# Attention with seven instead of eight lead steps, and its shared units at other places

## The reference

```
x = x + tanh(g_xattn) * attention(layernorm(x), ctx)     # x: 8 x 512 x 256, ctx: 8 x 512 x 192
x = x + tanh(g_ffn)   * ffn(layernorm(x))
attention: q, k, v = projections; s = clip(q k^T / 4, -1e4, 1e4); softmax(s) v; @ Wo + bo
ffn: gates = logits * (logits >= kth); h = gelu(x w1 + b1); y = h w2 + b2; out = sum_e y_e gates_e
```

## Time and profile before

| | us |
|---|---|
| median of three runs | 1897.73 |
| lowest and highest | 1895.09, 1897.74 |
| profiled execution, its own time | 1896.23 |
| its span | 1894.4 |
| attention in it | 93.0 to 516.1 |
| TensorE, VectorE, ScalarE busy over the span | 1862.6, 1291.1, 1277.7 |

### The profile page before, as it was taken

One profiled execution on the slowest core, in us unless ns is written; L12 is line 12 of the kernel. 1 busy time (PEld: TensorE's weight loads), 2 busy tenths in 40 slices (PEclk: granted clock), 3 DMA queues, 4 the chain that ended last, 5 costly groups with the idle time before them and its releaser, 6 DMA issues.

```text
span 1894.4 us, 25738 instructions
## 1 busy us (share of the span) xinstructions
PE 1862.6 (98%) x8868; PEld 1349.0 (71%) x8868; DVE 1291.1 (68%) x2279; ACT 1277.7 (67%) x2145; POOL 146.9 (8%) x327
## 2 busy tenths in 40 slices
PE   7999999999999999999999999999999999999998
PEld 6844444444478777887888788788878888887886
DVE  6789999999666665656556666755665676556555
ACT  4447778777855556767666676766667676666665
POOL 6201101111135200000000000000000000000000
PEclk9969999999999999999999999999999999999999
DMA  8933333233113254333232333233233423222321
GB/s 284 374 81 84 87 91 88 79 88 110 38 50 129 107 210 151 119 117 110 90 111 89 133 138 124 95 112 112 89 112 129 151 93 117 111 90 89 121 101 58
DMA packets 97245, 220.84 MB, mean 117 GB/s; under 512 B 31314, under 2 KB 49492, under 8 KB 87892
## 3 DMA queue, kind: packets, MB, share of 16 engines
q1 hardware_dynamic: 97108, 219.12, 33.5%
HBM read 178.57 MB, written 40.24 MB: 116 GB/s over the span
## 4 chain that ended last, share of the span: by engine, by line
PE 89%; ACT 3%; DVE 2%; issue 1%; POOL 0%; ACTq 0%; DVEq 0%; POOLq 0%
PE ps_y L2169 32%; PE ps_h L2116 28%; PE ps_t L862 7%; PE ps_o L873 6%; PE ps_h L2089 5%; PE ps_y L2101 4%; PE ps_s L851 2%; PE ps_m L898 2%; PE ps_m L884 1%; ACT w_raw L1170 1%; DVE low L1007 1%; PE ps_m L890 0%; ACT gelu L2366 0%; PE ps_m L919 0%; PE ps_m L905 0%
## 5 line engine op out<-in xcount | busy, mean ns | idle before, releaser
L2469 DVE TENSOR_TENSOR h_lo<-gelu,h_hi 128x512 fp32r<-128x512 f32 x512 | 352.8, 693 | 437.0 <-ACT h_hi L2369 405.7
L2116 PE MATMUL ps_h<-x_hi,w_pair 128*128 128x512 f32 x1568 | 562.3, 392 | 1.8 <-ACT gelu L2366 0.8
L2366 ACT ACTIVATE gelu<-early,b 128x512 f32<-128x512 f32 x336 | 243.2, 724 | 229.5 <-DVE early L2618 220.7
L2116 PEld LDWEIGHTS ps_h<-x_hi,w_pair 128*128 128x128 f32 x1568 | 294.3, 188 | 78.3 <-issue 6.0
L1007 DVE TENSOR_REDUCE low<-ps_s 128x1 f32<-128x512 f32 x512 | 322.1, 681 | 26.1 <-PE ps_s L851 23.1
L2369 ACT ACTIVATE h_hi<-gelu 128x512 fp32r<-128x512 f32 x448 | 283.5, 633 | 41.9 <-ACT gelu L2366 1.1
L2116 PE MATMUL ps_h<-x_lo,w_pair 128*128 128x512 f32 x784 | 309.4, 395 | 0.0
L2618 DVE TENSOR_TENSOR early<-ps_h,copy 128x512 f32<-128x512 f32 x336 | 230.5, 686 | 49.4 <-PE ps_h L2116 49.4
L1170 ACT ACTIVATE probs_T<-ps_t 128x512 f32<-128x512 f32 x384 | 206.4, 594 | 45.5 <-PE ps_t L862 44.6
L851 PE MATMUL ps_s<-k_st,q_st 48*128 48x512 f32 x512 | 205.0, 481 | 3.2 <-SPq L755 2.0
L2169 PE MATMUL ps_y<-h_hi,w_lo 128*128 128x512 f32 x512 | 202.7, 396 | 0.0
(11 more groups left out here) (263 smaller groups left out, 2536.4 us busy)
## 6 DMA issues: line engine op xcount, KB each, us to landing
x_hi<-blocks_scratch SPq DMA_DIRECT2D x28, 1024.0 KB, 5.2
x_lo<-blocks_scratch SPq DMA_DIRECT2D x28, 1024.0 KB, 8.8
x_hi<-blocks_scratch SPq DMA_DIRECT2D x28, 768.0 KB, 6.7
x_lo<-blocks_scratch SPq DMA_DIRECT2D x28, 768.0 KB, 10.2
gate<-gates_scratch SPq DMA_DIRECT2D x64, 256.0 KB, 3.2
q_st<-q_scratch SPq DMA_DIRECT2D x192, 64.0 KB, 2.3
k_st<-k_scratch SPq DMA_DIRECT2D x192, 64.0 KB, 2.3
k_scratch<-k_hl SPq DMA_DIRECT2D x8, 1024.0 KB, 5.6
```

Source lines behind the costliest of these rows:

```text
L2116: mm = pe.matmul(bank, w[wp], x[xp], start=start and n == 0, stop=n == 2, skip_group_check=not start)
L2366: act.activation(gelu[:, c % GELUS, :], src, ACT.Gelu_apprx_tanh, bias=b1[p][:, j:j + 1]).then_inc(gelu_done, 1)
L2469: dve.tensor_tensor(h_lo[:, j % RING, :], gelu[:, j % GELUS, :], h_hi[:, j % RING, :].bitcast(F32), ALU.subtract).then_inc(h_ready, 1)
```

## The change

`LEAD_STEPS` goes from 8 to 7, and all four tables are rewritten. The split y unit is gone: `HALVES` is empty. The kinds and numbers of units are the same.

```
-    (0, 0, 2): ("low", 0, 1), (0, 1, 2): ("out", -1, 3), (0, 2, 2): ("rows", -1, 0), (0, 2, 3): ("rows", -1, 1),
...
+    (0, 1, 1): ("low", 0, 1), (0, 2, 1): ("out", -1, 3), (0, 3, 1): ("rows", -1, 0), (1, 0, 2): ("rows", -1, 1),
+    (1, 1, 0): ("y", -1, 0), (1, 2, 0): ("y", -1, 1), (1, 2, 2): ("low", 0, 2), (2, 0, 1): ("out", 0, 0),
...
-HALVES = {(0, 3, 2): ("y", -1, 0)}
+HALVES = {}
...
-LEAD_STEPS = 8
+LEAD_STEPS = 7
```

More of the change, by code:

```diff
@@ L546 @@
+    (1, 1, 0): ("y", -1, 0), (1, 2, 0): ("y", -1, 1), (1, 2, 2): ("low", 0, 2), (2, 0, 1): ("out", 0, 0),
+    (2, 1, 1): ("x2T", -1, 0), (2, 2, 1): ("low", 0, 3), (2, 2, 3): ("x2T", -1, 1), (2, 3, 2): ("out", 0, 1),
+    (3, 0, 0): ("xnT", -1, 0), (3, 1, 1): ("xnT", -1, 1), (3, 1, 3): ("logits", -1, 0), (3, 2, 2): ("low", 1, 0),
+    (3, 3, 1): ("out", 0, 2), (3, 3, 3): ("pick", -1, 0),
 }
-HALVES = {(0, 3, 2): ("y", -1, 0)}
+HALVES = {}
 VECTOR_AT = {
[L551 to L556, removed]
+    (0, 2, 2): [("out", -1, 3)], (0, 3, 2): [("check", 0, 1)], (1, 1, 0): [("y", -1, 0)], (1, 1, 2): [("check", 0, 2)],
+    (1, 2, 0): [("statistics", -1, 0), ("statistics", -1, 1), ("y", -1, 1)], (1, 2, 1): [("statistics", -1, 2)],
+    (1, 3, 0): [("statistics", -1, 3)], (2, 0, 2): [("out", 0, 0)], (2, 1, 3): [("norm", -1, 0)], (2, 2, 1): [("norm", -1, 1)],
+    (2, 2, 2): [("check", 0, 3)], (2, 2, 3): [("norm", -1, 2), ("norm", -1, 3)], (2, 3, 1): [("out", 0, 1)],
+    (3, 0, 2): [("xnT", -1, 0)], (3, 1, 0): [("xnT", -1, 1)], (3, 1, 2): [("check", 1, 0)], (3, 3, 1): [("out", 0, 2)],
+    (3, 3, 3): [("pick", -1, 0)],
@@ L557 @@
 }
 SCALAR_AT = {
[L560 to L563, removed]
+    (0, 0, 3): [("copy", -1, 3)], (0, 1, 3): [("low", 0, 1)], (0, 3, 0): [("rows", -1, 0)], (1, 0, 2): [("rows", -1, 1)],
@@ L564 @@
+    (1, 0, 3): [("copy", 0, 0)], (1, 2, 0): [("low", 0, 2)], (2, 0, 3): [("copy", 0, 1)], (2, 1, 2): [("x2T", -1, 0)],
+    (2, 2, 1): [("low", 0, 3)], (2, 2, 3): [("x2T", -1, 1)], (3, 0, 0): [("xnT", -1, 0)], (3, 0, 3): [("copy", 0, 2)],
+    (3, 1, 0): [("xnT", -1, 1)], (3, 1, 3): [("logits", -1, 0)], (3, 2, 2): [("low", 1, 0)],
 }
 V_PLACE = 3
-LEAD_STEPS = 8
+LEAD_STEPS = 7
 SHARED_ORDER = [SHARED[at] for at in sorted(SHARED)]
```

## The result

The changed kernel takes 1900.24 us (median of 18 runs, 1897.06 to 1902.78), the kernel before, timed in turn with it, 1897.12 (18 runs, 1894.53 to 1899.62). The ratio is 1.0017, with a 95% interval of 1.0011 to 1.0023: slower by about 3 us, less than half of the 8.5 us that I forecast, though inside the range. The profiled execution took 1901.11 us (before 1896.23). Its span is 1899.2 us (1894.4).

A forecast was written before the change was run, and what follows sets the result against it. VectorE was taken to bound attention: busy 47.5 us of a 50.6 us steady batch, the rest waits. -1.7 (start) + 6 x 1.5 (batches 1 to 6) + 1.2 (last) = +8.5 us, median about 1906; range 1889 to 1914.

The forecast's parts named there:

- The start: Attention's prologue: one step of 2.4 us less, but batch 1 only 1.7 us earlier because of the low clock.
- the walk: Place-by-place pricing of a steady attention batch in the new order, summing VectorE's idle time to 4.64 us against 3.1.
- Both of my readings: Prologue clock: returns at the same time as now (taken, -1.7), or follows the joint steps, 0.8 us better.
- A steady batch: Attention batches 1 to 6: 52.1 us each instead of 50.6, 1.5 us more, as VectorE waits longer.
- (0,2) and (0,3), up to (1,0,0): Steps with out on TensorE and VectorE, and rows0: VectorE idle 0.16 within and 0.35 at (1,0,0).
- (2,2,0) and (3,0,1): VectorE idle 0.27 at (2,2,0), since x2T0 lengthens (2,1) with one norm beside it, and 0.06 at (3,0,1).
- xnT 1, before L1091: Second xnT unit at (3,1,0): the subtraction waits for TensorE's write and ScalarE's copy, VectorE newly idle 0.64 us.
- last pair to another kind of work 0.43 (0.33 in a chain): TensorE price: time from the last score pair to other work, 0.43 us, or 0.33 in a chain.
- The last batch: End of attention: ninth joint step costs about 3.1 us, the tail loses 1.9; net +1.2 us.
- That the waits stay (1): Rival, 17%: steady batch stays at 50.6 us, only the ends change; 1896.4 to 1897.7 us.
- That spread units give waits back (2): Rival, 17%: rows and y, no longer packed, are absorbed in the three banks; about -4 us, 1893 to 1894.
- That lowest rows come late (3): Rival, 8%: late landings at (1,2,2) and (3,2,2) delay TensorE over 1 us each; +15 on top, near 1920.

The follow-up runs named there:

- Experiment 2: Changed kernel with eight lead steps instead of seven, the new tables kept; ratio 1.0030 to the kernel before.
- experiment 9: Kernel before, eight lead steps and old tables, with only low 1 moved from (0,0,2) to (0,1,0); ratio 1.0007 to the kernel before.
- experiment 1: Changed kernel with the last batch's first expert weights converted one step later; 1897.54 us against 1895.94 for the kernel before, ratio 1.0009.
- Experiment 7: Changed kernel with first expert weights one step later and the second xnT unit served one place later; median 1897.27 us, ratio 1.0001 to the kernel before.
- experiments 6 and 8: 6: changed kernel, second xnT served one place later, ratio 1.0017. 8: the same plus first expert weights later and y 0 in halves, ratio 1.0009.
- experiment 5: Seven lead steps with the old tables, low 1 moved to (0,1,0) and the check of low 3 to (2,1,0); ratio 1.0006 to the kernel before.

## Why the prediction came out right in sign and wrong in size

The sign is less of a success than it looks. By the line that I drew ("slower over 1901.5") 1900.24 counts as no change, to which I had given 0.23, against 0.62 for slower.

**The start, forecast -1.7, measured -2.6.** The first exponential comes 2.38 us earlier, as said (2.4). Batch 1 starts 2.6 us earlier at an equal end of the low clock, 3.9 in the two profiles. Experiment 2 parts the two changes: the new places give 1.0 us in batch 0 and the lead the remaining 1.6. So the -1.7 for the lead was near, and the walk had left out batch 0's own gain. Both of my readings, a clock that returns at a fixed time and one that follows the joint steps, started from one execution of before. The end of the low stretch varies by 4.3 us between two executions of that kernel, which is worth 1.4 us at batch 1, more than the 0.8 between the readings. The Trainium skill, "TensorE: Matmul & The Clock Gate", Part 1, says that the point at which the clock rises differs from run to run of one kernel, and puts it at about half a microsecond. These traces agree that it differs, but by more: two profiles of one kernel differ by 3.4 us in the stretch's length, and the measurement decides.

**A steady batch, forecast +1.5, measured +0.6; this is the failing step.** The term that was mis-sized is the walk's sum of VectorE's waits, 4.64 us, of which 3.6 were measured. The direction and most places were right. Place by place, medians of five steady batches of after:

| waits of VectorE | walk | measured |
|---|---|---|
| (0,0) and (0,1), the pure boundaries | 0.48 | 0.58 |
| (0,2) and (0,3), up to (1,0,0) | 0.51 | 0.07 |
| rows 1, before L1007 at (1,1,0) | 0.67 | 0.61 |
| y 0, before L1040 | 1.25 | 1.18 |
| y 1, (1,2,0) and (1,3,0) | 0.46 | 0.31 |
| (2,2,0) and (3,0,1) | 0.33 | 0.04 |
| xnT 1, before L1091 | 0.64 | 0.34 |
| logits, (3,2,0) and (3,3,0) | 0.30 | 0.47 |

The price behind the two largest misses is "last pair to another kind of work 0.43 (0.33 in a chain)". The trace says when which holds. Distance from the last pair of a run to a unit of transposes or to pv behind it, in the steady batches:

| pairs in the run | before | after | with the pairs ahead | with 0.43 throughout |
|---|---|---|---|---|
| one (median) | 0.43 | 0.43 | 0.43 | 0.43 |
| two (median) | 0.33 | 0.33 | 0.67 | 0.76 |
| three, where nothing else is waited for | 0.33 | 0.33 | 0.90 | 1.00 |

So a run of pairs costs 0.24 us for each pair and 0.19 once; 0.33 at its start and 0.43 at its end count part of that twice. TensorE of after in the step (0,3), two runs of two:

```profile
319.99 0.50 PE L862 MATMUL ps_t<-q_st,k_st 49*128 49x512 f32 x1
...
320.32 0.39 PE L862 MATMUL ps_t<-q_st,k_st 49*128 49x512 f32 x1
...
320.65 0.66 PE L890 MATMUL ps_m<-ident,attn 128*128 128x128 f32 x4
321.24 0.50 PE L862 MATMUL ps_t<-q_st,k_st 49*128 49x512 f32 x1
...
321.57 0.39 PE L862 MATMUL ps_t<-q_st,k_st 49*128 49x512 f32 x1
...
321.90 1.05 PE L873 MATMUL ps_o<-probs_T,v_st 128*17 128x512 f32 x8
...
322.88 0.50 PE L862 MATMUL ps_t<-q_st,k_st 49*128 49x512 f32 x1
```

From 319.99 to 322.88 are 2.89 us; by my prices 0.33 + 0.43 + 0.59 + 0.33 + 0.43 + 0.98 = 3.09. Against VectorE's 2.57 the 3.09 gives about the 0.51 that I counted at (0,3). The 2.83 that the prediction writes beside it would have given 0.26: its line does not add up. In the same way 3.09 for (2,1), with one norm (0.40) beside the reductions, gives about the 0.27 at (2,2,0). At the shorter length of the steps both waits all but go, 0.4 and 0.3 us. At xnT 1 the run of two takes another 0.1. The other 0.2 there is ScalarE's copy, which I priced at 0.90 behind the transposes; in after it starts at 0.70:

```profile
302.15 0.66 PE L911 MATMUL ps_m<-ident,xn_b 128*128 128x128 f32 x4
...
302.85 0.60 ACT L1198 ACTIVATE x_hi<-ps_m 128x512 fp32r<-128x512 f32 x1
```

So 0.8 us of the miss is the price of a run, 0.2 the copy. The smaller ones at rows 1, y 0 and y 1 (0.3 together) and the waits that came out dearer (0.1 and 0.2) about cancel; their causes I have not looked into. No experiment varied the price of a run alone; it is read from both kernels, and experiment 9, which cuts one run in two, fits it. The Trainium skill, "TensorEngine Tiling (Array Packing)", Key Properties, says that a change of tiling mode drains TensorE. The trace agrees that leaving the pairs costs time, 0.43 or 0.33 instead of the 0.24 between pairs; the page has no figure.

**The last batch, forecast +1.2, measured +1.6 without the fall, +3.8 with it.** Without the wait before the logits it would be +0.4 (experiment 1, 48.87 against 48.45), so the tail was priced 0.8 too dear, and that 1.2 came near 1.6 is luck. What the walk missed is `first_weights`, 3.75 us of VectorE's work in the batch's last group, which no table lists. The logits moved from (3,3,0), behind it with slack, to (3,1,3), where they wait 1.2 us for a subtraction queued behind it. The prediction named what is queued behind waits in steady batches, but did not go through VectorE's stream of the last batch by itself.

**The rivals.** That the waits stay (1) did not occur, 3.6 us against 3.1. That spread units give waits back (2) did not, on balance: the emptied steps (0,2), (0,3) and (1,0) shrink from 10.25 to 8.80 us, but (1,2), with y 1 and low 2, grows from 2.93 to 4.89 and (3,1), with xnT 1 and the logits, from 2.93 to 4.25. (Two sums of the rivals do not come out: for the second the three waits named give 1.86 us and not 2.1, and the upper end of the first is 1897.73 - 0.5 = 1897.2, not 1897.7.) That lowest rows come late (3) did not, but the cover is thinner than I wrote. The profile puts the idle time ahead of the first L862 of a batch or group down to them, seven times in after and never in before:

```profile
260.10 0.18 PEld L862 LDWEIGHTS ps_t<-q_st,k_st 49*128 49x128 f32 x1 [0.85 <-DMA q_st<-low_rows]
```

Nothing is lost by it: a weight load stands idle for 0.85 us behind every pv, and L862 follows this pv by 0.98 us as elsewhere. The rows landed by 259.3 us, 4.0 after they were turned (255.32), where I had counted 3.5, since ScalarE copied them only at 256.60. Of the 4.8 us between, 0.8 is left.

**How the terms add up.** -2.6 + 3.5 + 1.6 + 0.5 = +3.0 us at an equal clock, against -1.7 + 9.0 + 1.2 = +8.5. All of the 5.5 us between them are the steady batches; the other three misses, -0.9, +0.4 and +0.5, cancel, which is luck. The 0.5 us behind attention goes with the new tables: all profiles with them and without a fall have 1379.4 to 1379.6 from the last exponential to the end, those with the old tables 1378.9 to 1379.0 (1379.2 with y 0 whole). Why, I have not explained.

No kernel here beats the one before. Experiment 7 equals it by the ratio, but at the same mean clock it is 1.4 us slower.

## What to carry to other kernels

Where two engines are both close to full, a wait in the trace is not a price: taking 0.34 or 0.86 us of wait away (experiments 6 and 8) moved it to the instruction behind or ahead and gained nothing. Price a reordering by the engine's own start-to-start distances, and read such a distance for each context in which it occurs, since 0.1 us too much at each of several places was here most of the error. Go through the first and the last pass of a pipeline by themselves: work that stands in no table is queued there, and a unit moved closer to it waits for it. Before two kernels are called equal, compare runs of the same mean clock: experiment 9 is 0.07% slower by its ratio, and 3.1 us (0.16%) when so compared.

## What the runs showed of the hardware that I had not expected

The low clock at the beginning of attention lasted 23.9, 27.3, 30.7 or 34.1 us, in kernels with either lead, and two profiles of the same kernel differ by 3.4 us of it. Each us by which it ends later starts batch 1 0.33 us later, so this alone moves a run by over a microsecond, as much as the terms in dispute. It is not chance alone: ten of eleven runs of experiment 5 and seven of ten of experiment 9 have a mean clock of 0.992, of before in the same sets 5 of 33 and 4 of 19. What in those kernels shortens it these runs don't show. A second fall, of 6.8 us in after and of 10.2 in experiment 2, came in the thin last batch; the same kernel with the same wait of 1.18 us ahead of it went without. It cost about 2.1 us in after's batch 7 (52.24 against 50.09). What decides it these runs don't show.
